# The weighted sums of a dense graph attention: features as TensorE weights, or weights of the edges as TensorE weights

## What is computed

```python
ft = jnp.einsum('nhd,od->nho', hv, W)
a1 = jnp.sum(ft * attn_l, axis=-1)
a2 = jnp.sum(ft * attn_r, axis=-1)
e = jax.nn.leaky_relu(a1[src] + a2[dst], negative_slope=NEG_SLOPE)
m = jax.ops.segment_max(e, dst, num_segments=N)
w = jnp.exp(e - m[dst])
denom = jax.ops.segment_sum(w, dst, num_segments=n)
alpha = w / jnp.maximum(denom[dst], 1e-16)
agg = jax.ops.segment_sum(alpha[:, :, None] * ft[src], dst, num_segments=n)
```

## Time and profile before

| | us |
|---|---|
| median of three runs | 4402.19 (4397.08 to 4413.13) |
| the profiled execution, time | 4392.1 |
| its span, first to last instruction | 4390.5 |
| TensorE busy with matmuls | 3893.2 (89%) |
| VectorE busy | 2024.6 (46%) |
| ScalarE busy | 1552.3 (35%) |
| POOL busy | 1536.1 (35%) |
| mean granted TensorE clock | 0.933 of 2.4 GHz |

### The profile page before, as it was taken

The page is one execution under the profiler, slowest core; times in us unless marked ns, Lnnn a source line. Parts: engine busy times, 40 slices in busy tenths (PEclk is TensorE's granted clock), DMA queues, the critical chain, the costliest instruction groups (busy, mean ns, idle before and its releaser), DMA issues. The chain is left out here.

```text
span 4390.5 us, 57679 instructions
## 1 busy us (share of the span) xinstructions
PE 3893.2 (89%) x18441; PEld 2974.4 (68%) x18453; DVE 2024.6 (46%) x2795; ACT 1552.3 (35%) x2608; POOL 1536.1 (35%) x1191
## 2 busy tenths in 40 slices
PE   8998655999997869849999899999999999989979
PEld 4554324776767869722222389999999999965579
DVE  6337877666633343477877333322233322012224
ACT  1111014666662312137878323333333333300021
POOL 4888831444430000101111134444444444346600
PEclk9999876999998879978989899999999999999989
DMA  4342102343323231232212245555555554368821
GB/s 133 102 113 51 13 5 63 63 87 61 55 46 107 82 107 52 87 103 40 54 36 42 82 140 179 181 194 184 176 178 176 187 193 136 111 216 268 261 82 64
DMA packets 296918, 495.26 MB, mean 113 GB/s; under 512 B 159297, under 2 KB 175704, under 8 KB 296807
## 3 DMA queue, kind: packets, MB, share of 16 engines
q1 hardware_dynamic: 208678, 218.04, 17.2%
q0 software_dynamic: 53568, 181.40, 14.5%
q10 hardware_dynamic: 34560, 94.45, 6.1%
HBM read 365.96 MB, written 127.48 MB: 112 GB/s over the span
## 5 line engine op out<-in xcount | busy, mean ns | idle before, releaser
L1751 PE MATMUL ps<-wsplit,xsplit 128*128 x6840 | 1235.6, 337 | 1.3 <-POOL xsplit L1718 1.3
L1751 PEld LDWEIGHTS ps<-wsplit,xsplit 128*128 128x128 f32 x6840 | 1180.1, 188 | 1.5 <-issue 1.5
L1191 ACT ACTIVATE work<-ps,work 128x418 f32<-128x418 f32 x720 | 435.5, 606 | 357.2 <-PE ps L1112 336.5
L1054 DVE SCALAR_TENSOR_TENSOR work<-work,cnt 128x1250 f32<-128x1250 f32 x240 | 367.9, 1533 | 338.5 <-ACT work L1191 305.0
L1150 PE MATMUL ps<-hbuf,work 128*128 128x193 f32 x2400 | 497.6, 346 | 13.2 <-DVE work L1071 13.2
L1718 POOL TENSOR_TENSOR xsplit<-ct,xsplit 128x768 fp32r<-128x768 f32 x190 | 369.0, 1942 | 298.3 <-ACTq L1783 298.2
L1688 DVE CAST wsplit<-wplain 128x768 fp32r<-128x768 f32 x204 | 114.6, 562 | 760.9 <-PE ps L1751 742.4
L1150 PEld LDWEIGHTS ps<-hbuf,work 128*128 128x128 f32 x2400 | 387.8, 192 | 83.8 <-issue 83.8
L1182 ACT ACTIVATE ps<-work,lr 128x418 f32<-128x418 f32 x720 | 417.7, 605 | 23.5 <-DMA work<-lrow_d 23.5
L1788 ACT ACTIVATE ct<-ps,invs 128x768 f32<-128x768 f32 x190 | 171.5, 903 | 710.3 <-PE ps L1751 710.3
L1139 PE MATMUL ps<-work,hbuf 128*65 128x512 f32 x720 | 374.3, 606 | 37.5 <-ACT work L1200 27.5
(11 more groups left out here) (207 smaller groups left out, 4286.0 us busy)
## 6 DMA issues: line engine op xcount, KB each, us to landing
wplain<-in_L_gnn_W_rel SPq DMA_DIRECT2D x34, 2304.0 KB, 9.5
msg_d<-ct ACTq DMA_DIRECT2D x190, 384.0 KB, 2.6
work<-lrow_d SPq DMA_DIRECT2D x48, 625.0 KB
feat_d<-work ACTq DMA_DIRECT2D x30, 386.0 KB
hbuf<-feat_d SPq DMA_DIRECT2D x12, 965.0 KB
gat_d<-work POOLq DMA_DIRECT2D x12, 960.0 KB
xplain<-gat_d SPq DMA_DIRECT2D x30, 384.0 KB
work<-xa_d SPq DMA_DIRECT2D x27, 384.0 KB
```

Of the source, the lines that this page charges most:

```text
L1054: v.scalar_tensor_tensor(p[:, 0:N], p[:, 0:N], 1.0, cnt3[:, q % NT, 0:N], ALU.min, ALU.mult).then_inc(self.s_p, 1)
L1191: act.activation(self.p[q % 3][:, c0:c1], ps[:, b, 0:c1 - c0], ACT.Exp, bias=self.l2[:, col:col + 1], scale=1.0 - SLOPE)\
L1751: last = pe.matmul(ps[:, 4 + 2 * (u % 2) + h, 0:HALF], x[:, u, c * P:(c + 1) * P], w[:, bass.ds(base + (c * D + h * HALF), HALF)], start=( ...
```

## The change

In `att2` the sums are taken as in `att0`: each 128 targets of p are held as weights and the 65 feature columns are moved, ten products a step instead of three. The sums come with targets on the partitions at once, five target tiles to a bank (325 columns), in two banks. There are two such pairs of banks, 3 and 4 for even heads, 5 and 6 for odd ones (`first_bank`), so a head waits for the eviction of the head before the last. `sums_out`, `turn_back`, the buffer `flat` and two semaphores are gone. The adds of step q+2 stand behind the second, fifth and eighth product of a step, as in `att0`. The eviction comes at step 1 of the next head instead of step 3, and the statistics two steps earlier with it. The products stay in fp32, and `att0` is not changed.

```diff
--- before.py
+++ after.py
@@ -872,7 +872,7 @@
                                                                          ("features_in", 3), ("head_stored", 2))),
                     *(sem(f"att_{n}") for n in (
                         "columns_ready", "maxima_taken", "shift_ready", "shift_stored", "relu_ready", "shift_added", "exp_ready",
-                        "weights_ready", "summed", "sums_free", "head_ready", "sums_copied", "turned_back", "banks_primed")))
+                        "weights_ready", "summed", "sums_free", "head_ready", "banks_primed")))
 
         class Attention:
 
@@ -886,7 +886,8 @@
                 self.C, self.mask, self.columns, self.outs, self.isolated = C, mask, columns, outs, isolated
                 self.narrow = C < P
                 self.banks = 2 if self.narrow else 5
-                self.b0 = 6 if self.narrow else 3
+                self.sets = 2 if self.narrow else 1
+                self.b0 = 3
                 self.tpb = NT // self.banks
                 cv = Carve(work, WORK)
                 if self.narrow:
@@ -899,7 +900,6 @@
                 self.junk = cv(N)
                 self.o = [cv(NT * C) for _ in range(2)]
                 if self.narrow:
-                    self.flat = cv(NP)[0:C + 1, :]
                     self.feat = lambda h, s: ft[:, s, h * (C + 1):(h + 1) * (C + 1)]
                 else:
                     h5 = Carve(hbuf, NT * (D + 12))
@@ -921,8 +921,13 @@
                 if not self.narrow:
                     self.at = {n: 0 for n in self.at}
                 (self.rows, self.s_L, self.s_R, self.s_c_in, self.s_feat, self.s_stored, self.s_cols, self.s_max, self.s_c, self.s_c_out,
-                 self.s_relu, self.s_add, self.s_exp, self.s_p, self.s_agg, self.s_free, self.s_out, self.s_flat, self.s_back,
+                 self.s_relu, self.s_add, self.s_exp, self.s_p, self.s_agg, self.s_free, self.s_out,
                  self.s_primed) = att_sems
+
+            def first_bank(self, h):
+
+
+                return self.b0 + self.banks * (h % self.sets)
 
             def row(self, v):
                 return lrow_d[v:v + NT, :].rearrange("j p -> (j p)")[0:N].partition_broadcast(P)
@@ -1054,15 +1059,13 @@
                     v.scalar_tensor_tensor(p[:, 0:N], p[:, 0:N], 1.0, cnt3[:, q % NT, 0:N], ALU.min, ALU.mult).then_inc(self.s_p, 1)
 
                 def evict(h):
-                    if self.narrow:
-                        v.wait_ge(self.s_back, h + 1)
-                    else:
-                        v.wait_ge(self.s_agg, self.at["agg"] + NT * (h + 1))
+                    v.wait_ge(self.s_agg, self.at["agg"] + NT * (h + 1))
                     if h >= 2 and self.narrow:
                         v.wait_ge(s_cols6, h - 1)
                     elif h >= 2:
                         v.wait_ge(self.s_stored[h % 2], self.at["stored"] + 16 * (h // 2))
-                    acc = ps[:, self.b0:self.b0 + self.banks, 0:self.tpb * (C + 1)].rearrange("p b (t c) -> p b t c", c=C + 1)
+                    b0 = self.first_bank(h)
+                    acc = ps[:, b0:b0 + self.banks, 0:self.tpb * (C + 1)].rearrange("p b (t c) -> p b t c", c=C + 1)
                     den = self.den.rearrange("p (b t) -> p b t", b=self.banks)
                     o = self.o[h % 2].rearrange("p (b t c) -> p b t c", b=self.banks, c=C)
                     step(v.tensor_scalar(den, acc[:, :, :, C], TINY, None, ALU.max if self.narrow else ALU.add))
@@ -1081,7 +1084,7 @@
                 v.sem_inc(self.s_cols, 1)
                 for t in range(NT + self.AHEAD):
                     maximum(t)
-                late = 3 if self.narrow else 0
+                late = 1 if self.narrow else 0
                 for q in range(NT * H):
                     weigh(q)
                     maximum(q + NT + self.AHEAD)
@@ -1114,16 +1117,6 @@
 
                     return [lambda b=b, c0=c0, c1=c1: piece(b, c0, c1) for b, (c0, c1) in enumerate(self.CUTS)]
 
-                def turn_back(h):
-                    pe.wait_ge(self.s_flat, 3 * (h + 1))
-                    if h:
-                        pe.wait_ge(self.s_free, self.at["free"] + self.banks * h)
-                    for dt in range(NT):
-                        b, t = divmod(dt, self.tpb)
-                        last = pe.transpose(ps[:, self.b0 + b, t * (C + 1):(t + 1) * (C + 1)], self.flat[:, dt * P:(dt + 1) * P],
-                                            ident[0:C + 1, 0:C + 1])
-                    last.then_inc(self.s_back, 1)
-
                 def total(q):
                     h, s = divmod(q, NT)
                     adds = add(q + 2)
@@ -1131,23 +1124,11 @@
                     if s == 0 and not self.narrow:
                         pe.wait_ge(self.s_feat[h % 3], 16 * (h // 3 + 1))
                     pe.wait_ge(self.s_p, self.at["p"] + q + 1)
-                    if self.narrow:
-                        for k, n0 in enumerate(range(0, NP, 512)):
-                            n1 = min(NP, n0 + 512)
-                            if s == 0 and h:
-                                pe.wait_ge(self.s_flat, 3 * (h - 1) + k + 1)
-                            last = pe.matmul(ps[0:C + 1, 3 + k, 0:n1 - n0], self.feat(h, s), p[:, n0:n1], start=(s == 0), stop=(s == NT - 1))
-                            if k == 2:
-                                last.then_inc(self.s_agg, 1)
-                            adds[k]()
-                        if s == 1 and h:
-                            turn_back(h - 1)
-                        return
                     for dt in range(NT):
                         b, t = divmod(dt, self.tpb)
-                        if s == 0 and t == 0 and h:
-                            pe.wait_ge(self.s_free, self.at["free"] + self.banks * (h - 1) + b + 1)
-                        last = pe.matmul(ps[:, self.b0 + b, t * (C + 1):(t + 1) * (C + 1)], p[:, dt * P:(dt + 1) * P], self.feat(h, s),
+                        if s == 0 and t == 0 and h >= self.sets:
+                            pe.wait_ge(self.s_free, self.at["free"] + self.banks * (h - self.sets) + b + 1)
+                        last = pe.matmul(ps[:, self.first_bank(h) + b, t * (C + 1):(t + 1) * (C + 1)], p[:, dt * P:(dt + 1) * P], self.feat(h, s),
                                          start=(s == 0 and t == 0), stop=(s == NT - 1), skip_group_check=True)
                         if dt == NT - 1:
                             last.then_inc(self.s_agg, 1)
@@ -1163,8 +1144,6 @@
                         piece()
                 for q in range(NT * H):
                     total(q)
-                if self.narrow:
-                    turn_back(H - 1)
 
             def act(self, act):
                 H = self.H
@@ -1191,14 +1170,6 @@
                     act.activation(self.p[q % 3][:, c0:c1], ps[:, b, 0:c1 - c0], ACT.Exp, bias=self.l2[:, col:col + 1], scale=1.0 - SLOPE)\
                        .then_inc(self.s_exp, 1)
 
-                def sums_out(h):
-                    act.wait_ge(self.s_agg, self.at["agg"] + NT * (h + 1))
-                    if h:
-                        act.wait_ge(self.s_back, h)
-                    for k, n0 in enumerate(range(0, NP, 512)):
-                        n1 = min(NP, n0 + 512)
-                        act.activation(self.flat[:, n0:n1], ps[0:self.C + 1, 3 + k, 0:n1 - n0], ACT.Copy).then_inc(self.s_flat, 1)
-
                 act.wait_ge(self.s_primed, 6 if self.narrow else 3)
                 act.wait_ge(self.s_cols, self.at["cols"] + 1)
                 for b in range(3):
@@ -1210,10 +1181,6 @@
                     exponent(q, 2)
                     relu(q + 1, 1)
                     relu(q + 1, 2)
-                    if self.narrow and q >= NT and q % NT == 1:
-                        sums_out(q // NT - 1)
-                if self.narrow:
-                    sums_out(H - 1)
 
         att0 = Attention(D // 4, mask1v, [((2 * l * 4 + h) * NT, ((2 * l + 1) * 4 + h) * NT) for l in range(3) for h in range(4)],
                          [(gat_d[l], h) for l in range(3) for h in range(4)], False)
```

## The result

The changed kernel takes **4653.91 us** (median of four runs, 4643.80 to 4664.70) against 4407.66 for the kernel before (four runs, 4397.08 to 4425.16): ratio 1.0555, 95% interval 1.0508 to 1.0602. The forecast was 4637, slower.

A forecast was written before the change was run, and what follows sets the result against it. TensorE, bound by loads at 1.2 GHz throughout (0.82): 118 steps at 6.20 us plus 9.2 make the stage 740.8 against 503.8, +237.0, less 2.3 at the end; 4627 profiled, 4637 us on the median's base, range 4585 to 4680.

The forecast's parts named there:

- The step at 1.2 GHz: Second attention: 20 loads at 0.214 us plus three adds at 0.64 give 6.20 us a step, as before; stage 740.8 us.
- The load of 128 fp32 columns: TensorE, each product's weights: transposes' spacing plus the record difference, 0.111 us at 2.4 GHz and 0.214 at 1.2.
- B: Rival, second attention: 1.2 GHz but loads keep 0.111 us; steps 4.16 us, stage 496, time 4392 us; chance 0.05.
- C: Rival, second attention: load and move one after the other at 1.2 GHz; steps 8.03 us, time 4857 us; chance 0.03.
- The clock: Second attention: starts at 1.2 GHz and stays there, since a new step moves 2600 cycles instead of 5120.
- fall behind each long wait: Old form of the second attention: its clock was said to fall behind each long wait.
- The step at 2.4 GHz: Second attention: 20 loads at 0.111 us plus three adds at 0.43 give 3.51 us a step, against 3.41 before.
- rival A: Second attention: clock rises and stays at 2.4 GHz; stage 431 us, change -75, time 4327 us; chance 0.10.
- VectorE's burst at a head's end: In rival A's stage, VectorE's work at a head's end adds about 1 us a head.
- Nothing for the copies, transposes and the moved eviction: Second attention: removed waits and moved eviction expose no lateness on ScalarE or VectorE; removed copy and transposes save 2.3 us at the end.
- The base: Whole kernel: profiled execution forecast at 4627 us, put at 4637 on the runs' median, which lay 10.1 higher.
- the 94 us: Old second attention: 120 undisturbed steps of 3.41 us would be 409 us; 94 are lost, much where a head ends.

The follow-up runs named there:

- e4: Changed kernel, each product of the second attention holding only 64 of its 128 targets as weights, the other sums left out: 4400.96 us (before: 4408.77).
- e2: Changed kernel, products moving 100 feature columns instead of 65, the extra 35 not read: 4643.18 us (before: 4408.77).
- e1: Changed kernel plus five dense unread fp32 products (128 columns loaded, 512 moved) ahead of the second attention's first sums: 4639.17 us (before: 4408.77).
- e3: Changed kernel with the edits of e1 and e2 together (warm start, 100 columns moved): 4540.54 us (before: 4408.77), ratio 1.0305.
- e5: e3 plus one dense unread product before the sums of steps 2 and 3 of each head: 4301.05 us (before: 4367.42), ratio 0.9859.
- e9: e5 with the dense product at step 3 of each head only: 4295.79 us (before: 4356.21), ratio 0.9853.
- e10: Changed kernel with the eviction back at step 3 of the next head, statistics two steps later: 4588.52 us (before: 4356.21), ratio 1.0525.
- e11: Kernel before, plus six unread products at a head's end where TensorE waits for the copy of the sums: 4307.56 us (before: 4356.21), ratio 0.9883.
- e7: e3 with its five dense warm-start products using one row of 128: 4614.82 us (before: 4367.42), ratio 1.057.

## Why the prediction was right

*The step at 1.2 GHz* was 6.20 us by the sum and 6.21 in the trace; the stage 740.8 and 741.2. The load of 128 fp32 columns, put together from the transposes' spacing and the difference of two records (0.214 us), measured 0.213; e4 shows that it is the load and e2 that the move is hidden under it. The measured 0.213 excludes B, which needed a load that keeps its 0.111 us, and C, which needed 0.322 for a pair. Part of the agreement of 0.214 with 0.213 is luck. The spacing of 0.103 is a mean over nine distances, of which the first is 0.063 and the others 0.106 to 0.113; with the steady 0.108 the load would have come out at 0.219, and the stage 12 us longer, still inside the range. The Trainium skill's figure ("TensorE: Matmul & The Clock Gate", section "LDWEIGHTS (loading the stationary operand)": columns divided by 1.2 in ns, 107 ns for 128) lies near the spacing at 2.4 GHz in e1 and e3, 0.111 to 0.112 us, and at half of this stage's 0.213 at 1.2.

*The clock.* The forecast that it starts at 1.2 GHz and stays there held over all 741 us. Its ground, that the new step moves half as many columns in the same time, was an argument from few stretches. e1 shows the same from the other side: even without a single wait the new step lets the clock fall. e3 differs from e1 in nothing but 100 columns instead of 65, and kept the clock for 43 steps, through two waits of 0.56 us, until the third; e5 and e9 kept it to the end. So what is moved between the loads decides here. Whether e5 and e9 kept the clock because a wait is filled or because the dense products move much themselves was not told apart, nor was the 65-column form run with fills.

One sentence of the prediction on this is wrong: the old form did not fall behind each long wait. It has eleven waits of 2.50 us for the copy, and behind ten of them the clock fell; it stayed at 1.00 through the one that ended at 2126.80:

```profile
2091.50:2166.20 74.70, 67.05 (x193) 17.60 (x193) 67.30 (x94) 65.08 (x123) 11.05 (x6) 1.00 0.24 53
```

*The step at 2.4 GHz*, 3.51 us, measured 3.44 and 3.49 in e1, and 3.58 with 100 columns, where by my estimate 3 x 0.029 us belong to the longer last moves: 3.49. Even with the clock the new form has no cheaper step than the old one's 3.41; its gain lies at the head's end. Nothing reached rival A's stage, 431 us with 65 columns; the nearest is e9 with 100 columns and fills, 439.4. VectorE's burst at a head's end, put at 1 us there, measured 1.07 in e3 (steps of 3.84 and 4.39 where 3.58 is undisturbed). The prediction's remark that six activations of some 0.6 us fill no whole step does not add up, for they come to 3.6 and the step is 3.41. The records overlap: ScalarE's busy time without the copies (395.8 - 14.6 us) is 3.2 us a step. At 6.21 us a step this had no bearing on the forecast.

*Nothing for the copies, transposes and the moved eviction* held: TensorE has no wait for ScalarE or VectorE left in the stage, and e10 gives the same stage with the eviction at its old place. The end gave 5.4 us instead of 2.3.

*The base.* The median lies 17 us above the forecast, inside the range. The profiled execution lies 19 above its 4627: 22.1 for the later start, 3.1 less at the end, 0.4 in the stage. On the chip of e10 this form of the stage lies 232 us above the kernel before, on the first chip 246; the stage itself gives 237 less 2.3. The rest I take for the spread of stages that the change does not touch; it is larger than what the stage's sum is off by, so that the median comes this near is luck where the stage's length is not.

The prediction left open where most of the 94 us go that the old stage loses against its undisturbed step. e11 gives 46.6 us of them back without touching any wait's cause: half of the 94 us was the low clock behind the waits. The waits for the copy are 27.5 of the rest.

The turned products can make the stage shorter: 439.4 us in e9, 64 less than the old 503.8, but only in a kernel that holds the clock. And 46.6 of these 64 us the old form gets as well once its waits are filled (e11). What is left for turning the products round is 17.8 us of stage, or 11.8 us of time on the same chip (4307.56 and 4295.79).

## What to carry to other kernels

Where small products are turned round so that the large operand is held and the small one moved, price a pair by its load, at both clock levels, and look for what will keep the clock: a TensorE that is 100% busy with loads and short moves ran at half clock here for 741 us. Moves can be widened under their loads at little cost (0.18 us a step at 1.2 GHz, 0.09 at 2.4), and a wait can be filled with a dense product that nobody reads. Here neither helped alone: the width without a warm start left the stage at 760.6 us, with it at 642.1, and with the fill at 439.4. Try the fill on the old form first: it was worth 46.6 us of stage there, the restructuring 17.8 more. Where a stage's end waits repeat, read the granted clock of the steps behind them before blaming the wait.

## What the runs showed of the hardware

- Products with a load of 128 fp32 columns and a short move come every 0.213 us at 1.2 GHz and every 0.111 to 0.112 at 2.4 (e1, e3). With 64 columns loaded it is 0.107 to 0.108 at 1.2 GHz, where the move may bound them; the load's record is 227 ns instead of 333 (e4). Transposes that load 128 fp32 columns come every 0.11 us at 1.2 GHz and every 0.06 at 2.4.
- The clock rose during five fp32 products of 512 columns over 128 rows, 6.58 us in all; over 8.74 us of the same five over one row it did not (e1, e7).
- It fell during products of 65 columns with no wait at all (e1). In a stream of 100 columns it was lost behind a wait of 0.56 us, after two equal waits in earlier heads had not cost it (e3); with one dense product a head it stayed for 439 us (e9).
- In a stream of 512-column moves, eight waits of 0.90 us did not cost the clock (e11), and waits of 2.50 us did ten times in eleven (the kernel before).
